# Placing of tokens split in two and moved within its round; GpSimd's list scatters read the tables themselves and are spread anew

## The chip, the cores and the metric

One core of a Trainium2 chip runs the whole program. The metric is device time in microseconds (us), the median of several executions. The engines are TensorE (PE), VectorE (DVE), ScalarE (ACT), GpSimd (POOL) and SyncE (SP); each runs its own program in order, and they meet at semaphores.

## What is computed

The input x has 16 x 512 tokens of 256 channels. All of it is normalised; then one branch is an RWKV layer over the 16 sequences of 512 tokens, the other a routed mixture of experts, and the output is x + s * silu(g).

```
def _L0_attn_ref(x, ...):
    x = _ln(x, ln0_w, ln0_b)
    h = _ln(x, ln1_w, ln1_b)
    xx = _time_shift(h)
    xk = h * tmk + xx * (1 - tmk)          # xv, xr alike
    k = jnp.einsum('btc,oc->bto', xk, Wk)  # v alike, sr with a sigmoid
    att = _wkv(w, time_first, k, v)        # recurrence over time
    x = x + jnp.einsum('btc,oc->bto', sr * att, Wo)
    h2 = _ln(x, ln2_w, ln2_b)
    ...
    kf = jnp.square(jax.nn.relu(jnp.einsum('btc,hc->bth', xk2, Wfk)))
    kv = jnp.einsum('bth,ch->btc', kf, Wfv)
    return x + jax.nn.sigmoid(...) * kv

def _L0_ffn_ref(x, Wg, W1, W2):
    probs = jax.nn.softmax(xt @ Wg, axis=-1)
    _, top_idx = jax.lax.top_k(probs.T, cap)     # each expert takes its best T // E tokens
    tok2exp = ...                                # one expert for each token
    for e in range(E):
        h = jax.nn.gelu(xt @ W1[e], approximate=False) @ W2[e]
        out = out + gate[:, None] * h
```

## The kernel before

The work goes in two stages. The first runs 16 rounds b = 0 to 15, one for each sequence of 512 tokens, and computes the RWKV layer; the second works off 72 tiles of 128 tokens, sorted by expert.

**A round.** On TensorE (`round_`, L936) round b does the hidden products of sequence b-1 (`hidden`, L887, lines 901, 903 and 908, eight groups of six), its `receptance` (L920, two halves), `turn1` of b+1 (transposes, L836), `channel_out(b-1, 0)` (L932), `project_out(b)` (L883), the projections k and v of b+1 (L871), another `channel_out`, `turn2(b)`, the projection r of b+1, and two more `channel_out`. `hidden` waits from its fourth group on for ScalarE's `relu` of three groups earlier; the second half of `receptance` waits for `relu` 6; `channel_out(b-1, 0)` waits for all eight squares.

On ScalarE (`round_`, L644) the order is: `logs(b)` (L599), relus and squares 0 and 1 and relu 2 of b-1 (L621, L625), `shares(b)` (L605, L608, with a load of function tables), relus 3 and 4, square 2, relu 5, `norm1(b+1)` (L530), relu 6, square 3, relu 7, squares 4 to 7, `affine1(b+1)`, and later `norm2(b)`, `norm0(b+2)`, `affine2(b)` (L538), `exp_past(b+1)`, `exponents(b+1)`, `split_mix(b)` and `exp_now(b+1)`. `norm1(b+1)` waits for GpSimd's `rstd1(b+1)`, `norm2(b)` for `rstd2(b)`.

On VectorE (`round_`, L1529, and `wkv`, L1449):

```
def wkv(b, extra, ahead, further):
    wkv_state(b)              # L1398, scans; ScalarE's logs wait for them
    embed_scale(b + 1); embed_shift(b + 1)
    extra(b, 0)
    wkv_gap(b)                # L1405; ScalarE's shares wait for it
    gate_out(b - 2); moments1(b + 1); residual2(b - 2)
    wkv_mix(b)                # L1416 to L1445, its end releases project_out
    extra(b, 1); fetch(b + 2)
```

(shortened) and then `mix1(b+1)`, `residual1(b)` with the second statistics (L1475, L1320, L1324), `extra(b, 2)`, `mix1_r(b+1)`, `wkv_start(b+1)` (L1384 to L1392), `extra(b, 3)` and `mix2(b)` (L1337, L1341, L1376). `extra` is a slot for the router's work, of which each round has four.

**Routing.** Rounds 0 to 3 take the logits and the softmax, rounds 3 to 11 search each expert's threshold bit by bit; round 11 (`SELECT_ROUND`) counts ties, selects, chooses an expert for each token, and keeps the prefix sums. In round 12 (`LIST_ROUND`), slot 0, `place_tokens` (L1239 to L1291) turns them into the row of the sorted list that each token takes: `place` (128 x 64) and `info` (128 x 64 x 4), and it ends by raising `routed`. `list_part` (L1294) then copies a quarter of both tables, 16 columns, to `place_cur` and `info_cur` (L1299, L1300), and again in slot 0 of rounds 13, 14 and 15, where it first waits until the scatters of the quarter before have landed.

**GpSimd.** Its round (L446) computes the reciprocal deviations of the norms, `rstd1(b+1)` and `rstd2(b)` (L426 to L431, four small instructions each), which wait for the statistics on VectorE. From round 12 on, `add_to_list` (L413) issues indirect DMAs (L419), each of which scatters one column of 128 tokens into `sorted_list` in HBM. There are 64. The order of rounds 12 to 14 is `rstd1(b+1)`, eight scatters, `rstd2(b)`, eight scatters; that of round 15 is sixteen scatters, `zero_rows` (L443, eight memsets, after a wait for the last `att_done`), `rstd2(15)`. Then come the gathers of the second stage.

**SP.** It issues the loads and stores of the rounds; after `routed` it loads W2, after all 64 scatters it loads the list back (L367) and then W1. VectorE's `first_indices` (L1519) waits for the list in round 15.

Of the kernel before, what the change touches and what calls it, by code (L numbers as in the profile page):

```python
# [28 lines left out]
I32 = mybir.dt.int32  # L29
F32R = mybir.dt.float32r  # L30
ALU = mybir.AluOpType
ACT = mybir.ActivationFunctionType
AX_X = mybir.AxisListType.X
ds = bass.ds

P = 128
# [34 lines left out]
def rwkv_times_moe(nc, x, xT, vec, ln0_w, ln0_b, WkT, WvT, WrT, WoT, WfkT, WfrT, WfvT, Wg, W1, W2,  # L71
# [19 lines left out]
    with ExitStack() as ctx:  # L91
# [19 lines left out]
        def sb(name, shape, dt=F32):  # L111
            return ctx.enter_context(nc.sbuf_tensor(name, shape, dt))
# [20 lines left out]
        place_cur = sb("place_cur", [P, LT], I32)  # L133
        info_cur = sb("info_cur", [P, LT, 4], I32)
# [103 lines left out]
        probs_turned routed pads_out list_cur list_scattered list_in w1_in w2_in w2_hi_done w2_first_done w2_split  # L238
# [140 lines left out]
        def _(pool):  # L379
# [33 lines left out]
            def add_to_list(b, half):  # L413

                wait_run(pool, S["list_cur"], b - (LIST_ROUND - 1))
                if isinstance(b, int) and b == LIST_ROUND:
                    pool.wait_ge(S["pads_out"], 16)
                for j in range(half * LT // 2, (half + 1) * LT // 2):
                    pool.indirect_dma_start(sorted_list[:, :], bass.IndirectOffsetOnAxis(place_cur[:, j:j + 1], axis=0),  # L419
                                            info_cur[:, j, :], None).then_inc(S["list_scattered"], 16)  # L420
# [25 lines left out]
            def round_(b, listing=False, ahead=True):  # L446
                if ahead:
                    rstd1(b + 1)
                if listing:
                    add_to_list(b, 0)  # L450
                if not ahead:
                    add_to_list(b, 1)
                    zero_rows()
                rstd2(b)
                if listing and ahead:
                    add_to_list(b, 1)
# [9 lines left out]
            round_(LIST_ROUND, listing=True)  # L466
            with pool.Fori(LIST_ROUND + 1, NB - 1) as b:
                round_(b, listing=True)
            round_(NB - 1, listing=True, ahead=False)
# [572 lines left out]
        def _(v):  # L1042
# [128 lines left out]
            def route(b, point):  # L1171
                if b == SELECT_ROUND:
                    (count_ties, select, choose, keep_prefix)[point]()
                elif point == 0:
                    place_tokens()
                    list_part(b)
# [62 lines left out]
            def place_tokens():  # L1239
# [7 lines left out]
                c8 = lambda k: tiny[:, 16 + k * E:16 + (k + 1) * E]  # L1247
# [10 lines left out]
                R.then(v.tensor_scalar(c8(5), c8(4), float(P), -1.0, ALU.mult, ALU.add))  # L1258

                R.then(v.tensor_tensor(work, work, logits, ALU.subtract))  # L1260
# [33 lines left out]
            def list_part(b):  # L1294

                n = b - LIST_ROUND
                if not (isinstance(b, int) and b == LIST_ROUND):
                    wait_run(v, S["list_scattered"], n * (16 * LT))
                v.tensor_copy(place_cur[:], place[:, ds(n * LT, LT)])  # L1299
                v.tensor_copy(info_cur[:].rearrange("p t w -> p (t w)"),  # L1300
                              info[:].rearrange("p t w -> p (t w)")[:, ds(n * (4 * LT), 4 * LT)].bitcast(I32)
                              ).then_inc(S["list_cur"], 1)

            def listing(b, point):
                if point == 0:
                    list_part(b)

# [263 lines left out]
            with v.Fori(LIST_ROUND + 1, NB - 2) as b:  # L1571
                round_(b, listing)
            round_(NB - 2, listing, further=False)
            round_(NB - 1, listing, ahead=False, further=False)
# [114 lines left out]
```

## Time and profile before

| | |
|---|---|
| runs shown, us | 1118.58, 1117.18, 1118.22 (median 1118.22) |
| profiled execution, us | 1113.32 |
| its span on the core, us | 1111.4 |
| mean granted TensorE clock | 0.978 of 2.4 GHz |
| TensorE busy | 92% |
| VectorE busy | 81% |
| ScalarE busy | 62% |
| GpSimd busy | 35% |

The profiled execution lies 4.9 us under the median. Its span runs from the first to the last instruction; 1.9 us of its time lie around the span. In the timeline a row gives the start and the length of one or more like instructions, and in brackets the idle time of the engine before them and who ended it. The ends of matmuls are modelled. The first stage ends near 812 us, the second fills the rest.

### The profile page before, as it was taken

The numbers are of one execution on the slowest core, as the hardware profiler recorded it, in microseconds if no ns is written. First come the engines' busy times: TensorE is split into PE (matmuls) and PEld (weight loads), VectorE is DVE, ScalarE is ACT, GpSimd is POOL, SyncE is SP. The second block draws the span as 40 slices with busy tenths as digits, with TensorE's granted clock in tenths as the row PEclk, the third lists the DMA queues.
The fourth block names the chain that finished last, engine by engine and source line by source line (L and its number), as shares of the span: only waits on it lengthen the run. The fifth ranks groups of instructions, "written<-read, shape, count | busy, mean of one in ns | idle before, by whom it ended". The sixth has DMA issues, their size and how long they took to land.

```text
span 1111.4 us, 20678 instructions
## 1 busy us (share of the span) xinstructions
PE 1024.8 (92%) x5440; PEld 837.4 (75%) x5441; DVE 900.9 (81%) x1997; ACT 689.5 (62%) x1233; POOL 387.2 (35%) x407
## 2 busy tenths in 40 slices
PE   5679999999999999999999699999897999999996
PEld 5357787776777767777776578677787999999996
DVE  5799889998988989888899969787445777777775
ACT  2648565686756858567585557658254666666654
POOL 3105414110101101011110265467705665666663
PEclk9879999999999999999999899999998999999999
DMA  9424230101101011010110101063503333333320
GB/s 303 153 78 128 78 112 19 39 28 30 57 0 57 11 46 57 0 57 0 57 58 0 45 14 57 1 189 116 202 12 90 102 106 102 105 102 108 98 63 16
DMA packets 60091, 80.50 MB, mean 72 GB/s; under 512 B 7806, under 2 KB 47359, under 8 KB 60034
## 3 DMA queue, kind: packets, MB, share of 16 engines
q1 hardware_dynamic: 48658, 54.69, 15.5%
q0 software_dynamic: 11392, 25.32, 7.8%
q8 instruction: 19, 0.31, 0.1%
q14 instruction: 22, 0.18, 0.1%
HBM read 65.17 MB, written 26.49 MB: 82 GB/s over the span
## 4 chain that ended last, share of the span: by engine, by line
PE 59%; DVE 18%; issue 7%; ACT 7%; POOL 6%; another core or an unknown queue 1%; DVEq 1%; DMA 1%; ACTq 0%; POOLq 0%
PE psKV L932 13%; PE psM L1003 12%; PE psM L871 9%; PE psM L883 5%; POOL sorted_list L419 2%; DVE arena L1398 2%; PE psM L920 2%; DVE arena L1341 2%; PE psT L836 2%; ACT arena L625 2%; PE psR L792 2%; PE psM L901 2%; PE psM L1015 2%; DVE bnst L1320 2%; ACT arena L530 2%
## 5 line engine op out<-in xcount | busy, mean ns | idle before, releaser
L932 PE MATMUL psKV<-arena 128*128 128x256 f32 x1024 | 232.7, 382 | 4.1 <-ACT arena L625 4.1
L932 PEld LDWEIGHTS psKV<-arena 128*128 128x128 f32 x1024 | 193.1, 191 | 43.9 <-issue 17.5
L426 POOL TENSOR_SCALAR lnw<-mv 128x4 f32<-128x4 f32 x32 | 19.0, 593 | 509.6 <-DVE mv L1324 509.5
L1003 PE MATMUL psM<-arena 128*128 128x128 f32 x1152 | 143.4, 278 | 0.7 <-issue 0.2
L1003 PEld LDWEIGHTS psM<-arena 128*128 128x128 f32 x1152 | 135.8, 194 | 3.1 <-issue 2.6
L901 PE MATMUL psM<-mix_hi,wfk_hi 128*128 128x512 f32 x256 | 106.5, 416 | 21.8 <-ACT arena L621 21.6
L577 ACT ACTIVATE arena<-psM 128x512 f32<-128x512 f32 x64 | 36.5, 590 | 130.4 <-PE psM L871 130.4
L487 POOL DMA_INDIRECT out_dram<-arena,out_idx x72 | 90.8, 1261 | 76.1 <-DVE row_idx L1512 36.4
L1341 DVE SCALAR_TENSOR_TENSOR arena<-arena,vecs 128x512 f32<-128x512 f32 x160 | 109.9, 745 | 0.0
L530 ACT ACTIVATE arena<-s_ring,cf 128x256 f32 (+1 forms) x128 | 66.5, 592 | 58.0 <-POOL cf L431 58.0
L903 PE MATMUL psM<-mix_hi,wfk_lo 128*128 128x512 f32 x256 | 101.0, 395 | 0.0
L621 ACT ACTIVATE arena<-psM 128x512 f32<-128x512 f32 x128 | 73.9, 589 | 35.2 <-PE psM L908 32.7
L740 ACT ACTIVATE arena<-psM 128x512 f32<-128x512 f32 x72 | 43.1, 599 | 69.9 <-PE psM L1003 49.6
L419 POOL DMA_INDIRECT sorted_list<-info_cur,place_cur x64 | 75.6, 1182 | 22.3 <-issue 20.5
L908 PE MATMUL psM<-mix_lo,wfk_hi 128*128 128x512 f32 x256 | 80.1, 394 | 0.4 <-DVE mix_lo L1376 0.4
L901 PEld LDWEIGHTS psM<-mix_hi,wfk_hi 128*128 128x128 f32 x256 | 48.6, 190 | 37.5 <-ACT arena L621 27.9
L474 POOL DMA_INDIRECT arena<-xs_rows,row_idx x64 | 68.4, 1068 | 22.1 <-issue 22.1
L625 ACT ACTIVATE arena<-arena 128x512 f32<-128x512 f32 x128 | 75.4, 627 | 0.9
L1590 DVE TENSOR_TENSOR hT_rounded<-arena,hT_rounded 128x512 fp32r<-128x512 f32 x72 | 49.5, 687 | 28.4 <-ACT hT_rounded L741 19.8
L883 PE MATMUL psM<-wo,arena 128*128 128x256 f32 x256 | 60.0, 389 | 5.1 <-DVE arena L1445 5.1
L920 PE MATMUL psM<-arena 128*128 128x256 f32 x256 | 60.1, 382 | 3.8 <-ACT arena L621 3.8
L1337 DVE TENSOR_TENSOR arena<-arena 128x512 f32<-128x512 f32 x64 | 41.7, 688 | 24.9 <-ACT arena L538 20.3
(208 smaller groups left out, 2417.9 us busy)
## 6 DMA issues: line engine op xcount, KB each, us to landing
desk<-in_x SPq DMA_DIRECT2D x16, 512.0 KB, 5.0
arena<-in_x SPq DMA_DIRECT2D x16, 512.0 KB
desk<-in_xT SPq DMA_DIRECT2D x16, 512.0 KB, 4.0
xs_rows<-s_ring SPq DMA_DIRECT2D x16, 512.0 KB
xs_rows<-in_x SPq DMA_DIRECT2D x16, 512.0 KB
desk<-in_W SPq DMA_DIRECT2D x8, 512.0 KB
arena<-in_W SPq DMA_DIRECT2D x8, 512.0 KB
out_dram<-arena,out_idx POOLq DMA_INDIRECT x72
```

The costliest lines, as they stand in the source:

```text
L419: pool.indirect_dma_start(sorted_list[:, :], bass.IndirectOffsetOnAxis(place_cur[:, j:j + 1], axis=0), info_cur[:, j, :], None).then_inc(S ...
L487: pool.indirect_dma_start(out[:, :], bass.IndirectOffsetOnAxis(out_idx[i][:, 0:1], axis=0), out_t[i], None, bounds_check=T - 1, oob_is_err ...
L530: ins = act.activation(hn[:, j], xs[:, j * C:(j + 1) * C], ACT.Identity, scale=cf[:, 0, j:j + 1], bias=cf[:, 1, j:j + 1])
L625: act.activation(kf2[:, h], kf2[:, h], ACT.Square).then_inc(S["sq_done"], 1)
L871: ins = pe.matmul(psM[:, u % 3, :], w[:, k, c * P:(c + 1) * P], mixA[:, m, k, :], start=(k == 0), stop=(k == CH - 1))
L883: ins = pe.matmul(psM[:, 1 + j // 2, (j % 2) * C:(j % 2 + 1) * C], att[:, c, j * P:(j + 1) * P], wo[:, c, :], start=(c == 0), stop=(c == C ...
L901: pe.matmul(psM[:, h % 3, :], wfk_hi[:, k, n], mix_hi[:, k, :], start=(k == 0), stop=False)
L903: pe.matmul(psM[:, h % 3, :], wfk_lo[:, k, n], mix_hi[:, k, :], start=False, stop=False)
L920: ins = pe.matmul(psM[:, (HC + u) % 3, (j % 2) * C:(j % 2 + 1) * C], mixB_r[:, k, j * P:(j + 1) * P], wfr[:, k, :], start=(k == 0), stop=( ...
L932: ins = pe.matmul(psKV[:, j // 2, (j % 2) * C:(j % 2 + 1) * C], kf2[:, h, j * P:(j + 1) * P], wfv[:, h, :], start=(h == 0), stop=(h == HC ...
L1003: ins = pe.matmul(psM[:, i % 2, f * P:(f + 1) * P], w1_t[i % 2][:, k, f * P:(f + 1) * P], xnT[i % 2][:, k, :], start=(k == 0), stop=(k == ...
L1341: return v.scalar_tensor_tensor(dst[:, c], dmix[:, c], vecs[:, c, V[m]:V[m] + 1], hT[:, c, 0:SEQ], ALU.mult, ALU.add)
```

## The change

`place_tokens` is cut in two. `expert_starts`, its first part (to the subtraction at L1260), runs in slot 2 of round 12, behind `residual1(12)` and its statistics; the rest runs in slot 3, behind `mix1_r(13)` and `wkv_start(13)`, ahead of `mix2(12)`. The arithmetic is the same. `list_part` and its two small tables are gone, with the semaphore `list_cur` and VectorE's waits on landed scatters in rounds 13 to 15; each scatter takes its column from `place` and `info`. GpSimd's order becomes: round 12 `rstd1(13)`, `rstd2(12)`, a wait for `pads_out` and `routed`, 16 scatters; round 13 `rstd1(14)`, 8 scatters, `rstd2(13)`, 16 scatters; round 14 `rstd1(15)`, 8, `rstd2(14)`, 16; round 15 `zero_rows`, `rstd2(15)`.

```
-            def add_to_list(b, half):
-
-                wait_run(pool, S["list_cur"], b - (LIST_ROUND - 1))
-                if isinstance(b, int) and b == LIST_ROUND:
-                    pool.wait_ge(S["pads_out"], 16)
-                for j in range(half * LT // 2, (half + 1) * LT // 2):
-                    pool.indirect_dma_start(sorted_list[:, :], bass.IndirectOffsetOnAxis(place_cur[:, j:j + 1], axis=0),
-                                            info_cur[:, j, :], None).then_inc(S["list_scattered"], 16)
+            def add_to_list(first, last):
+
+                for t in range(first, last):
+                    pool.indirect_dma_start(sorted_list[:, :], bass.IndirectOffsetOnAxis(place[:, t:t + 1], axis=0),
+                                            info[:, t, :].bitcast(I32), None).then_inc(S["list_scattered"], 16)
...
-            def round_(b, listing=False, ahead=True):
+            def round_(b, mid=(0, 0), late=(0, 0), ahead=True):
                 if ahead:
                     rstd1(b + 1)
-                if listing:
-                    add_to_list(b, 0)
-                if not ahead:
-                    add_to_list(b, 1)
+                    add_to_list(*mid)
+                else:
                     zero_rows()
                 rstd2(b)
-                if listing and ahead:
-                    add_to_list(b, 1)
+                if isinstance(b, int) and b == LIST_ROUND:
+                    pool.wait_ge(S["pads_out"], 16)
+                    pool.wait_ge(S["routed"], 1)
+                add_to_list(*late)
...
-            round_(LIST_ROUND, listing=True)
-            with pool.Fori(LIST_ROUND + 1, NB - 1) as b:
-                round_(b, listing=True)
-            round_(NB - 1, listing=True, ahead=False)
+            q = NTILE // 8
+            round_(LIST_ROUND, late=(0, 2 * q))
+            round_(LIST_ROUND + 1, mid=(2 * q, 3 * q), late=(3 * q, 5 * q))
+            round_(LIST_ROUND + 2, mid=(5 * q, 6 * q), late=(6 * q, 8 * q))
+            round_(NB - 1, ahead=False)
...
                 if b == SELECT_ROUND:
                     (count_ties, select, choose, keep_prefix)[point]()
-                elif point == 0:
+                elif point == 2:
+                    expert_starts()
+                elif point == 3:
                     place_tokens()
-                    list_part(b)
...
+            def expert_starts():
+                v.wait_ge(S["route_pe"], 4)
+
+                R.then(v.tensor_copy(et(logits), psR[:].rearrange("p (t e) -> p e t", e=E)))
+                R.wait()
+                R.then(v.tensor_tensor_scan(work, reset, logits, 0.0, ALU.mult, ALU.add))
...
+                R.then(v.tensor_scalar(c8(5), c8(4), float(P), -1.0, ALU.mult, ALU.add))
+                R.then(v.tensor_tensor(work, work, logits, ALU.subtract))
+
             def place_tokens():
...
-                R.then(v.tensor_tensor(work, work, logits, ALU.subtract))
                 R.wait()
...
-            def list_part(b):
-
-                n = b - LIST_ROUND
-                if not (isinstance(b, int) and b == LIST_ROUND):
-                    wait_run(v, S["list_scattered"], n * (16 * LT))
-                v.tensor_copy(place_cur[:], place[:, ds(n * LT, LT)])
-                v.tensor_copy(info_cur[:].rearrange("p t w -> p (t w)"),
-                              info[:].rearrange("p t w -> p (t w)")[:, ds(n * (4 * LT), 4 * LT)].bitcast(I32)
-                              ).then_inc(S["list_cur"], 1)
-
-            def listing(b, point):
-                if point == 0:
-                    list_part(b)
-
+            def plain(b, point):
+                pass
...
             with v.Fori(LIST_ROUND + 1, NB - 2) as b:
-                round_(b, listing)
-            round_(NB - 2, listing, further=False)
-            round_(NB - 1, listing, ahead=False, further=False)
+                round_(b, plain)
+            round_(NB - 2, plain, further=False)
+            round_(NB - 1, plain, ahead=False, further=False)
```

## Rows read from the trace of the kernel before

**Rows 1.** The page: TensorE's busy line, and the group of the list's scatters.

```profile
PE 1024.8 (92%) x5440; PEld 837.4 (75%) x5441; DVE 900.9 (81%) x1997; ACT 689.5 (62%) x1233; POOL 387.2 (35%) x407
...
L419 POOL DMA_INDIRECT sorted_list<-info_cur,place_cur x64 | 75.6, 1182 | 22.3 <-issue 20.5
```

**Rows 2.** Timeline of TensorE, 600 to 800 us (start, us, what, idle before).

```profile
633.07 0.79 PE L901 MATMUL psM<-mix_hi,wfk_hi 128*128 128x512 f32 x1 [10.07 <-ACT arena L621]
...
638.35 3.68 PE L920 MATMUL psM<-arena 128*128 128x256 f32 x16
...
680.78 0.50 PE L901 MATMUL psM<-mix_hi,wfk_hi 128*128 128x512 f32 x1 [0.97 <-ACT arena L621]
...
683.66 3.62 PE L920 MATMUL psM<-arena 128*128 128x256 f32 x16
...
687.99 3.62 PE L932 MATMUL psKV<-arena 128*128 128x256 f32 x16
...
792.03 1.95 PE L836 MATMUL psT<-cst,arena 128*128 128x128 f32 x8 [4.12 <-ACT arena L530]
```

**Rows 3.** Windows: PE, PEld, DVE, ACT, POOL busy; granted clock; DMA share; GB/s.

```profile
633.00:639.00 6.00, 5.93 (x15) 4.71 (x16) 6.00 (x11) 5.00 (x11) 4.66 (x6) 0.54 0.68 201
```

**Rows 4.** Timeline of VectorE, 560 to 832 us.

```profile
617.66 0.68 DVE L1242 COPY desk<-psR 128x512 f32<-128x512 f32 x1
...
620.75 0.68 DVE L1260 TENSOR_TENSOR desk<-desk 128x512 f32<-128x512 f32 x1
...
627.65 0.15 DVE L1291 COPY desk<-desk 128x1 f32<-128x1 f32 x1
...
640.79 1.29 DVE L1445 SCALAR_TENSOR_TENSOR arena<-arena 128x512 f32<-128x512 f32 x2
...
645.13 2.73 DVE L1341 SCALAR_TENSOR_TENSOR arena<-arena,vecs 128x512 f32<-128x512 f32 x4
...
663.70 1.36 DVE L1337 TENSOR_TENSOR arena<-arena 128x512 f32<-128x512 f32 x2 [5.24 <-ACT arena L538]
...
669.01 2.34 DVE L1398 TENSOR_TENSOR_SCAN arena<-arena 128x512 f32<-128x512 f32 x2
...
677.59 0.38 DVE L1324 BATCH_NORM_AGGREGATE mv<-bnst 128x2 f32<-128x6 f32 x4
...
787.19 0.38 DVE L1324 BATCH_NORM_AGGREGATE mv<-bnst 128x2 f32<-128x6 f32 x4
```

**Rows 5.** Timeline of ScalarE, 600 to 730 us.

```profile
628.68 1.28 ACT L605 ACT_TABLE_LOAD   x1 [9.10 <-DVE arena L1405]
...
670.34 1.28 ACT L599 ACT_TABLE_LOAD   x1 [0.88 <-DVE arena L1398]
...
676.38 1.28 ACT L605 ACT_TABLE_LOAD   x1
...
682.11 2.08 ACT L530 ACTIVATE arena<-s_ring,cf 128x256 f32 x4
```

**Rows 6.** Timeline of GpSimd, 500 to 800 us.

```profile
640.81 1.50 POOL L419 DMA_INDIRECT sorted_list<-info_cur,place_cur  x1 [0.30 <-issue]
...
646.41 0.96 POOL L419 DMA_INDIRECT sorted_list<-info_cur,place_cur  x1 [0.30 <-issue]
...
698.37 0.49 POOL L426 TENSOR_SCALAR lnw<-mv 128x4 f32<-128x4 f32 x1 [4.44 <-DVE mv L1324]
...
703.50 1.16 POOL L419 DMA_INDIRECT sorted_list<-info_cur,place_cur  x1 [0.53 <-issue]
...
712.76 2.23 POOL L419 DMA_INDIRECT sorted_list<-info_cur,place_cur  x1 [0.31 <-issue]
...
723.41 0.96 POOL L426 TENSOR_SCALAR lnw<-mv 128x4 f32<-128x4 f32 x1 [8.42 <-DVE mv L1324]
...
726.11 0.20 POOL L431 TENSOR_TENSOR cf<-lnw,cf 128x4 f32<-128x4 f32 x1 [0.18 <-POOL cf L429]
...
787.93 0.25 POOL L426 TENSOR_SCALAR lnw<-mv 128x4 f32<-128x4 f32 x1
```

More of the change, by code:

```diff
@@ L132, in rwkv_times_moe @@
         stats_cur = sb("stats_cur", [P, J, 2])
-        place_cur = sb("place_cur", [P, LT], I32)
-        info_cur = sb("info_cur", [P, LT, 4], I32)
         bnst = sb("bnst", [P, J, 6])
@@ L237, in rwkv_times_moe @@
         var_ready pow_ready bit_step bit_counted bit_summed route_step route_pe route_exp_in route_exp_out
-        probs_turned routed pads_out list_cur list_scattered list_in w1_in w2_in w2_hi_done w2_first_done w2_split
+        probs_turned routed pads_out list_scattered list_in w1_in w2_in w2_hi_done w2_first_done w2_split
         x_in x_out s_out fetched x0_ready scaled0 embedded moments_step ln1_stats cf1_ready hn1_ready tr1_done
@@ L1237, in keep_prefix @@
                 assert R.k == R_KEPT, R.k
-            def place_tokens():
+            c8 = lambda k: tiny[:, 16 + k * E:16 + (k + 1) * E]
+            def expert_starts():
                 v.wait_ge(S["route_pe"], 4)
@@ L1245, in place_tokens @@
                 R.wait()
-                c8 = lambda k: tiny[:, 16 + k * E:16 + (k + 1) * E]
                 R.then(v.tensor_scalar(c8(0).bitcast(I32), et(work)[:, :, NTILE - 1], float(P - 1), None, ALU.add))
@@ L1260, in place_tokens @@
                 R.then(v.tensor_tensor(work, work, logits, ALU.subtract))
+            def place_tokens():
                 R.wait()
```

## The prediction

> **What bounds the kernel now.** I read the page first. TensorE is busy for 92% of the span [rows 1], so a round is worth what it makes TensorE stop for. Then the timeline of TensorE: in a common round it stops once, for 0.97 us in the hidden products, at 680.78; in round 12 it stops at the same place for 10.07 us, at 633.07 [rows 2]. ScalarE's timeline says why: its shares waited 9.10 us for VectorE's gap, L1405 [rows 5]. VectorE's says what stood ahead of the gap: the placing, 617.66 to 627.80 (L1242 to L1291) [rows 4]. The products behind the stop ran slow as well: from 633.07 to the receptance at 638.35 they took 5.28 us, where the same ones took 2.88 (680.78 to 683.66) [rows 2]; the granted clock there was 0.54, the lower of the two levels, 1.2 GHz, for most of the stretch [rows 3].
>
> All times below are on the axis of this trace; what is won in round 12 is taken off at the end.
>
> **1. What leaves slot 0 of round 12.** The stop shrinks from 10.07 to 0.97, 9.1 us, and the slow clock behind it goes, 5.28 - 2.88 = 2.4. Nothing else is late there: ScalarE was waiting for the gap alone, and the statistics and `norm1(13)` follow the gap as in a common round. **Gain 11.5 us.** Bounds: 9.1, if the clock falls for another cause, and 11.5.
>
> **2. What slots 2 and 3 get.** The first part lasts 617.66 to 621.43, 3.77 us, the rest 6.37 [rows 4]. VectorE has a hole there: it idled 5.24 us until 663.70, when `mix2(12)` began, so its work before ended at 658.46 [rows 4]. With 10.14 us put in, `mix2(12)` starts at 668.6, 4.9 late. `mix1_r` and `wkv_start(13)` slip by 3.8 at most; their readers (the r projection, `exp_past`) start from 661 on, so I cost that at nothing; were that cover gone it would be under 1 us. Behind `mix2` come the scans of `wkv_state(13)`, at 669.01 before, 673.9 now. ScalarE's logs begin 1.33 us behind them (670.34 [rows 5]), at 675.2, and its shares 6.04 behind that (676.38 [rows 5]), less some 0.5 of waits for TensorE, which is now ahead: 680.7. The seventh of the eight hidden groups waits for relu 3, which stands behind the shares, so TensorE resumes at 685.1 instead of 680.78: **4.3 us lost**; the late start of the hidden products, some 1.7 us, is within it. Bounds 3.3 (`affine2` could come earlier, and VectorE's hole with it) and 4.9.
>
> **3. GpSimd's queue behind `routed`.** `routed` rises at 668.6. Behind the wait stand 16 scatters, and behind these `rstd1(14)`, on which `norm1(14)` waits in the middle of ScalarE's relus and squares. A scatter costs 1.18 us and 0.30 between two, 1.48 [rows 1, 6]; the first starts 0.3 behind the signal. The sixteenth ends at 668.9 + 23.7 = 692.6. The statistics that `rstd1(14)` needs were there at 677.97 [rows 4], 682.9 now: GpSimd comes 10 us late. `rstd1` took 2.9 us beside a busy VectorE (723.41 to 726.31 [rows 6]); VectorE is nearly through by then, I take 2.6. `norm1(14)` starts at 695.3 instead of 682.11 [rows 5]. From `norm1` to `channel_out(12, 0)` it was 687.99 - 682.11 = 5.9 us, squares in between [rows 2, 5]; so TensorE reaches that product at 701.2 instead of 688.0, 13.2 late. It will have stopped for about 8 us ahead of the second half of `receptance`. A stop of 10.07 and one of 4.12 us were each followed by slow products (eight transposes in 1.95 us at 792.03) [rows 2], so the clock falls here too, on 2.6 us of work (half of `receptance`, `turn1`) that starts 3.5 us ahead of 701.2: 1.6 more. **Loss 14.8 us, with the 4.3 of step 2 in it.** Bounds: scatters undisturbed, 0.96 + 0.30 = 1.26 [rows 6], give 9.7 and 0 to 1 of clock; all at 1.50 + 0.30 give 18.3 and 2.
>
> **4. Rounds 13 and 14.** The list needs the same 64 scatters, but 16 late ones now stand between `rstd2(13)` and `rstd1(15)`. From the start of `rstd2(13)` to the first scatter it was 5.13 us (698.37, 703.50), eight scatters took 11.49 (703.50 to 714.99) [rows 6], so sixteen end 28.1 us after the start. `rstd1(15)` was due 25.04 after it (723.41): 3.1 late. `rstd1(14)` ended, a period of 45.24 us before 726.31 (the statistics at 677.97 against 723.2), at 681.07 and `norm1(14)` began at 682.11: 1.0 of slack. **2.1 lost**; bounds 0 (scatters at 1.26 end 25.3 after) and 5. The eight in the middle fit: `rstd2` follows `rstd1` by 20.2 us (678.2 to 698.37), and three and 11.5 are needed.
>
> **5. The end.** In round 15 the scatters, `zero_rows` and `rstd2(15)` (787.93 [rows 6]) followed each other; the second statistics were ready at 787.57 [rows 4], 0.36 us before. The last scatters now end near 772, and SP's list and W1 loads start some 7 us sooner, with nothing waiting for them. **Gain 0.3.** The six copies and three waits of `list_part` in rounds 13 to 15 lie in VectorE's spare time: nothing.
>
> Sum: -11.5 + 14.8 + 2.1 - 0.3 = **+5.1 us**. The sum stands on the profiled execution (1113.32 us, 1.9 around the span); it lies 4.9 under the median shown, and I carry the difference over: 1118.2 + 5.1 = **1123.3**. A measurement of this kernel can tell some 0.2% (2.2 us) from no change.
>
> **A rule against the trace.** A scatter took 0.96 us beside L1341 (646.41) but 1.50 beside L1445 (640.81), both with two inputs in SBUF [rows 4, 6]; the price thus hangs on the neighbour only in part, and the mean holds both. The Trainium skill, GPSIMD Engine Reference, Key points, says that GpSimd shares its SBUF interfaces with VectorE and that instructions with two SBUF inputs contend with it. By that rule alone nearly all of the 16 would be stretched. This trace bears it out in some rows and not in others.
>
> **Rivals.**
> - *The scatters run short.* Out of the new place many of them stand beside `mix2`, the embedding and the gap, where some were at 0.96. At 1.26 each: -11.5 + 9.7 + 1 + 0 - 0.3 = -1.1, so 1117.1. For it: the 0.96 at 646.41 [rows 6]. Against: `wkv_mix`, beside whose end the 1.50 stands, falls in the same stretch. Chance 0.22.
> - *Faster: GpSimd's queue does not reach the path.* The place is `norm1(14)`. If its coefficients come by 686.4 (682.11 + 4.3), only step 2 remains: -11.5 + 4.3 - 0.3 = -7.5, 1110.7 us. That takes 16 scatters in 686.4 - 2.6 - 668.9 = 14.9 us, 0.93 each; from there the price rises by 16 us for each us of a scatter, and even lies at some 1.28. No row has less than 1.26, which speaks against; but GpSimd's times are the roughest of the trace, and with scatters near 1.26, no fall of the clock and a smaller step 2 the time already lies 3 us below. Chance 0.18.
> - *Every scatter is stretched.* At 1.80 each step 3 costs 5.1 more (16 x 0.32) and step 4 some 3 more: +13, 1131 us. For it: rows at 1.50 [rows 6]; against: the rows at 0.96, and eight in 11.49. Chance 0.07.
> - *The forecast*, 0.53.
>
> **Numbers.** Slower by over 0.2%: 0.53 + 0.07 = 0.60; within: 0.22; faster: 0.18. The range leaves out the full price of the second rival and of the third. Its lower end is 1116.0 (scatters at 1.26 and no fall of the clock: -2.1), its upper 1127.5 (4.2 above the forecast: half of the way to the stretched scatters).
>
> **What the new profile would show.** Right: no stop of 10 us in round 12; VectorE without idle time ahead of `mix2(12)`; a stop of TensorE of 2 to 3 us ahead of the seventh hidden group of round 13; sixteen scatters in a row of about 23.7 us and `norm1(14)` idle for some 9 us with GpSimd's L431 as releaser; TensorE stopped about 8 us in `receptance` with a low granted clock behind it; one wait for L431 of 2 us in round 14. Wrong: sixteen scatters in under 19 us; `norm1(14)` waiting for nothing; or a stop in round 12 that stays, for then something else than the placing held the shares.

## The result, and the profile of the changed kernel

The changed kernel took 1129.07 us (median of 4 runs, 1127.15 to 1131.43), the kernel before 1118.4 (4 runs, 1117.18 to 1118.92): ratio 1.0096, with 95% confidence between 1.0074 and 1.0118. That is 10.7 us slower, where 5.1 were forecast. The profiled execution took 1127.15 us for a span of 1125.2, 13.8 more than the profiled execution of before.

From the page, answering to [rows 1]:

```profile
PE 1030.4 (92%) x5440; PEld 841.2 (75%) x5441; DVE 900.4 (80%) x1989; ACT 689.5 (61%) x1233; POOL 379.9 (34%) x407
...
L414 POOL DMA_INDIRECT sorted_list<-info,place x64 | 72.3, 1130 | 32.1 <-issue 18.7
```

A scatter is a little shorter than before (1130 against 1182 ns), and GpSimd has a new wait of 13.4 us (32.1 - 18.7) ahead of this group. TensorE is busy 5.6 us longer (1030.4 against 1024.8) for the same 5440 products, at a mean clock of 0.974 against 0.978; VectorE and ScalarE are not busy for longer. The rest of the 13.8 us is waits. The timeline of TensorE, 600 to 810 us, answering to [rows 2]:

```profile
624.24 0.50 PE L897 MATMUL psM<-mix_hi,wfk_hi 128*128 128x512 f32 x1 [0.99 <-ACT arena L617]
...
660.74 0.47 PE L897 MATMUL psM<-mix_hi,wfk_hi 128*128 128x512 f32 x1 [0.70 <-ACT mix_hi L610]
...
673.01 0.49 PE L897 MATMUL psM<-mix_hi,wfk_hi 128*128 128x512 f32 x1 [2.28 <-ACT arena L617]
...
687.37 3.74 PE L916 MATMUL psM<-arena 128*128 128x256 f32 x8 [8.04 <-ACT arena L617]
...
726.32 0.50 PE L897 MATMUL psM<-mix_hi,wfk_hi 128*128 128x512 f32 x1 [1.51 <-issue]
...
734.94 0.50 PE L897 MATMUL psM<-mix_hi,wfk_hi 128*128 128x512 f32 x1 [2.70 <-ACT arena L617]
...
802.17 1.09 PE L832 MATMUL psT<-cst,arena 128*128 128x128 f32 x8 [3.78 <-ACT arena L526]
```

Round 12 has only the common stop of 0.99 us at 624.24 left of the 10.07 at 633.07 before. In round 13 stand a stop of 2.28 us ahead of the seventh hidden group and one of 8.04 in `receptance`. Two further stops of over 1 us stand in round 14 (726.32 and 734.94). The last line is the end, 4.12 before and 3.78 now.

The windows of TensorE, answering to [rows 3] (columns: stretch; length and busy time of PE, PEld, DVE, ACT, POOL; granted clock; DMA share; GB/s):

```profile
633.00:639.00 6.00, 6.00 (x28) 5.08 (x27) 4.00 (x7) 1.14 (x3) 0.00 (x0) 1.00 0.01 1
682.00:692.00 10.00, 4.63 (x17) 3.80 (x18) 0.00 (x0) 5.63 (x11) 8.02 (x11) 0.66 0.02 1
732.00:737.00 5.00, 2.30 (x8) 1.64 (x7) 4.28 (x6) 5.00 (x10) 4.08 (x4) 0.83 0.96 287
737.00:740.00 3.00, 3.00 (x11) 2.42 (x10) 3.00 (x6) 2.75 (x6) 2.39 (x3) 0.71 1.11 369
```

The stretch of the axis that stood at 0.54 before now has the full clock. It holds other products now; the ones that ran slow before start at 624.24 and reach the receptance in 2.87 us (5.28 before). Three other stretches have lost the clock: behind the stops at 687 and 735, and behind the one at 673.01, where the products up to the receptance take 4.44 us in place of 2.88.

VectorE's timeline, 655 to 675 us, answering to [rows 4], and ScalarE's, 660 to 740 us, answering to [rows 5]:

```profile
656.92 0.15 DVE L1290 COPY desk<-desk 128x1 f32<-128x1 f32 x1
656.99 1.28 DVE L1324 TENSOR_TENSOR arena<-arena 128x512 f32<-128x512 f32 x2
...
670.44 0.38 DVE L1311 BATCH_NORM_AGGREGATE mv<-bnst 128x2 f32<-128x6 f32 x4
```

```profile
668.62 1.28 ACT L601 ACT_TABLE_LOAD   x1
...
684.77 2.07 ACT L526 ACTIVATE arena<-s_ring,cf 128x256 f32 x4 [10.33 <-POOL cf L426]
...
725.67 0.60 ACT L617 ACTIVATE arena<-psM 128x512 f32<-128x512 f32 x1 [4.57 <-PE psM L904]
...
727.73 0.60 ACT L617 ACTIVATE arena<-psM 128x512 f32<-128x512 f32 x1 [0.80 <-remote]
...
729.93 0.60 ACT L617 ACTIVATE arena<-psM 128x512 f32<-128x512 f32 x1 [0.94 <-remote]
```

GpSimd's timeline, 640 to 735 us, answering to [rows 6]:

```profile
657.97 1.39 POOL L414 DMA_INDIRECT sorted_list<-info,place  x1 [13.42 <-DVE desk L1290]
659.66 1.44 POOL L414 DMA_INDIRECT sorted_list<-info,place  x1 [0.30 <-issue]
661.41 2.63 POOL L414 DMA_INDIRECT sorted_list<-info,place  x1 [0.30 <-issue]
664.34 1.99 POOL L414 DMA_INDIRECT sorted_list<-info,place  x1 [0.30 <-issue]
666.63 0.96 POOL L414 DMA_INDIRECT sorted_list<-info,place  x1 [0.30 <-issue]
...
681.56 0.96 POOL L414 DMA_INDIRECT sorted_list<-info,place  x1 [0.30 <-issue]
682.59 0.20 POOL L421 TENSOR_SCALAR lnw<-mv 128x4 f32<-128x4 f32 x1
...
727.74 2.01 POOL L414 DMA_INDIRECT sorted_list<-info,place  x1 [0.30 <-issue]
729.82 0.20 POOL L421 TENSOR_SCALAR lnw<-mv 128x4 f32<-128x4 f32 x1
```

Placing ends at 657.07 and `mix2(12)` follows at once, with no idle time in between. Sixteen scatters then fill 657.97 to 682.52, and `rstd1(14)` stands behind them although its statistics were ready at 670.82 (670.44 + 0.38). So `norm1(14)` waits 10.33 us. The chain is as forecast. The new thing is at 725.67: ScalarE's first relu of round 14 waits 4.57 us, where in e8, another run of the same program, it waits 1.08 for the same products. The next two relus have waits with the releaser "remote", which stands here where the profile names no engine and no queue of the program.

**Counting by rounds.** The clearest measure is the distance between two starts of `residual1`'s addition on VectorE (L1475 before, L1462 after). All runs of this study stand in the table, each against the kernel before on its own chip. "Sum" is the sum of the four distances less 193.3, the sum of the profile of before.

```
run              chip  round 12  13     14     15     sum   us        before    ratio   95%
before           -     58.69     45.25  45.24  44.15  -     1118.4
changed          -     47.13     60.40  51.89  44.15  +10.2 1129.07   1118.4    1.0096  1.0074 to 1.0118
e5_before        4     58.80     45.23  45.23  44.17  +0.1  1091.31   (one run)
e1_again         15    47.16     61.87  46.24  44.15  +6.1  1094.0    1090.49   1.0033  1.0021 to 1.0044
e2_first16       15    47.12     60.07  45.20  44.19  +3.3  1093.78   1090.49   1.0031  1.0018 to 1.0043
e3_second16      15    47.13     50.19  46.23  44.18  -5.6  1083.92   1090.49   0.9933  0.9912 to 0.9954
e4_spread        15    47.14     50.35  45.19  44.22  -6.4  1081.62   1090.49   0.9919  0.9898 to 0.994
e6_slot0         4     57.49     49.43  46.26  44.17  +4.0  1093.93   1090.42   1.003   1.002 to 1.004
e7_slot0_spread  4     57.44     45.22  45.21  44.18  -1.3  1089.3    1090.42   0.9988  0.9975 to 1.0001
e8_again         4     47.13     61.15  46.23  44.20  +5.4  1093.92   1090.42   1.0028  1.0016 to 1.0039
e9_tiles_later   10    47.12     49.72  48.74  44.62  -3.1  1121.33   1125.14   0.9963  0.9942 to 0.9984
e10_spread2      10    47.12     50.37  47.26  44.17  -4.4  1122.15   1125.14   0.9977  0.9954 to 0.9999
e11_again        10    47.12     61.68  51.79  44.21  +11.5 1134.29   1125.14   1.0091  1.0068 to 1.0114
e12_exit13       2     47.13     60.85  47.89  44.18  +6.7  1096.89   1089.67   1.0068  1.0051 to 1.0084
e13_first16b     2     47.17     61.51  45.27  44.19  +4.8  1092.71   1089.67   1.0023  1.001 to 1.0036
e14_second16b    2     47.17     48.77  46.24  44.16  -7.0  1083.37   1089.67   0.9946  0.9924 to 0.9967
e15_exit13       5     47.16     60.57  47.88  44.17  +6.5  1096.52   1091.44   1.0047  1.0012 to 1.0082
e16_first16      5     47.12     60.46  45.20  44.18  +3.6  1095.15   1091.44   1.0032  1.0014 to 1.005
e17_tiles_later  12    47.14     50.76  47.30  51.92  +3.8  1122.82   1124.92   0.9981  0.995 to 1.0013
e18_exit13       12    47.17     61.27  47.90  44.21  +7.2  1128.69   1124.92   1.0046  1.0022 to 1.007
```

Two things are to be seen before any experiment is read. First, the kernel before takes about 1090 us on chips 15, 4, 2 and 5 and 1118 to 1125 on chips 10 and 12 and on the one of the forecast. Its rounds 12 to 15 are the same on both sorts (58.69 and 58.80, then 45.2). Second, a round's distance says more than the total: for one program it repeats within 0.1 us in round 12 and within 1.5 in round 13, where the clock moves it.

### The profile page after: what moved, and what is told of

It reads as the page before. It is cut to its first block, busy times and chain, and to the rows that moved or that the text cites. A ratio compares the mean times of both kernels' runs of the same rounds, so it can differ in the third digit from the quotient of the medians.

```text
span 1125.2 us, 20636 instructions
## 1 busy us (share of the span) xinstructions
PE 1030.4 (92%) x5440; PEld 841.2 (75%) x5441; DVE 900.4 (80%) x1989; ACT 689.5 (61%) x1233; POOL 379.9 (34%) x407
## 4 chain that ended last, share of the span: by engine, by line
PE 58%; DVE 18%; issue 11%; ACT 6%; POOL 4%; DMA 1%; another core or an unknown queue 1%; DVEq 1%; ACTq 0%; SPq 0%; POOLq 0%
PE psKV L928 12%; PE psM L999 10%; PE psM L867 9%; PE psM L879 5%; PE psM L916 2%; DVE arena L1385 2%; DVE arena L1328 2%; POOL sorted_list L414 2%; PE psT L832 2%; PE psR L788 2%; PE psM L897 2%; DVE bnst L1307 2%; PE psR L1011 2%; PE psM L1011 2%; PE psM L904 2%
## 5 line engine op out<-in xcount | busy, mean ns | idle before, releaser
L999 PEld LDWEIGHTS psM<-arena 128*128 128x128 f32 x1152 | 136.8, 194 | 5.3 <-issue 5.0
L414 POOL DMA_INDIRECT sorted_list<-info,place x64 | 72.3, 1130 | 32.1 <-issue 18.7
L1577 DVE TENSOR_TENSOR hT_rounded<-arena,hT_rounded 128x512 fp32r<-128x512 f32 x72 | 49.7, 690 | 36.2 <-ACT hT_rounded L737 19.9
L470 POOL DMA_INDIRECT arena<-xs_rows,row_idx x64 | 70.9, 1107 | 22.0 <-issue 19.7
L916 PEld LDWEIGHTS psM<-arena 128*128 128x128 f32 x256 | 49.1, 194 | 22.4 <-ACT arena L617 15.2
```

The lines of the kernel that those rows point to most:

```text
L916: ins = pe.matmul(psM[:, (HC + u) % 3, (j % 2) * C:(j % 2 + 1) * C], mixB_r[:, k, j * P:(j + 1) * P], wfr[:, k, :], start=(k == 0), stop=( ...
L999: ins = pe.matmul(psM[:, i % 2, f * P:(f + 1) * P], w1_t[i % 2][:, k, f * P:(f + 1) * P], xnT[i % 2][:, k, :], start=(k == 0), stop=(k == ...
```

## The experiments

The expectations use short names: Q is the forecast's account, that GpSimd's queue behind `routed` holds `rstd1`; the others are named in them.

**Is it the number of scatters ahead of `rstd1`?** e1 runs the changed kernel again. e2, e3 and e4 change nothing but where the list is split:

```
-            round_(LIST_ROUND, late=(0, 2 * q))
-            round_(LIST_ROUND + 1, mid=(2 * q, 3 * q), late=(3 * q, 5 * q))
-            round_(LIST_ROUND + 2, mid=(5 * q, 6 * q), late=(6 * q, 8 * q))
e2:
+            round_(LIST_ROUND, late=(0, 16))
+            round_(LIST_ROUND + 1, mid=(16, 24), late=(24, 32))
+            round_(LIST_ROUND + 2, mid=(32, 42), late=(42, 8 * q))
e3:
+            round_(LIST_ROUND, late=(0, 8))
+            round_(LIST_ROUND + 1, mid=(8, 16), late=(16, 32))
+            round_(LIST_ROUND + 2, mid=(32, 42), late=(42, 8 * q))
e4:
+            round_(LIST_ROUND, late=(0, 8))
+            round_(LIST_ROUND + 1, mid=(8, 19), late=(19, 31))
+            round_(LIST_ROUND + 2, mid=(31, 42), late=(42, 8 * q))
```

> The changed kernel once more, with nothing altered, to see what of its profile repeats. Time between two starts of the residual addition on VectorE (the round period; 45.25 us for rounds 13 and 14 of the kernel before): in the first profile of the changed kernel it was 60.4 us for round 13 and 51.9 for round 14. Theory Q (both losses come from GpSimd's queue: 16 scatters ahead of rstd1): 60.4 and 51.9 again, within 0.5. Rival F (the stall of 4.6 us of ScalarE at the start of round 14, for which the profile names no releaser behind its first wait, is a chance of one execution): 60.4, but round 14 at 47 or less. Median near 1129 us under Q; under F the profiled time would lie some 5 us under the other runs.

> The changed kernel, with 16 scatters ahead of rstd1(14) as it has them, but only 8 late ones in round 13 (8 ahead of rstd1(15)); the others moved to round 14. Q: round 13 stays at 60.4, round 14 falls from 51.9 to 45.3 to 46; in all some 6 us less than the changed kernel, 1122 to 1124. Rival F2 (round 14's loss is one of starting the program's code behind ScalarE's and VectorE's loops and has nothing to do with the scatters): round 14 stays near 51.9, no change in time.

> The changed kernel with 8 scatters ahead of rstd1(14) in place of 16, and 16 ahead of rstd1(15) as it has them. Q: rstd1(14) starts when its statistics are there; round 13 falls from 60.4 to 45.25 + 4.1 = 49.4, with the late start of the shares alone left; round 14 stays at 51.9; in all 11 us less than the changed kernel, near 1118. Rival P (the placing in slots 2 and 3 costs TensorE most of the 15 us of round 13 whatever GpSimd does): round 13 stays above 56. F2: as Q for round 13.

> The changed kernel with the scatters spread so that none stands in the way of a wanted rstd: 8 late in round 12, 11 and 12 in round 13, 11 and 22 in round 14. Q: round 13 at 49.4, round 14 at 45.3 to 46; time = before - 11.5 + 4.1 - 0.3, 7 to 8 us under the kernel before, 1110 to 1112. F2: round 14 near 51.9 and a time near 1117. P: no faster than before.

Measured: round 13 costs 60.07 and 61.87 us with 16 scatters ahead of `rstd1(14)` (e2, e1), and 50.19 and 50.35 with 8 (e3, e4). Round 14 costs 46.23 and 46.24 with 16 ahead of `rstd1(15)` (e3, e1), and 45.19 and 45.20 with 8 or 12 (e2, e4). With the rest of the change in all four kernels, each of the two places follows the scatters ahead of it, and Q holds for round 13: the second eight of the first sixteen are worth some 10 us. For round 14 it gives 1.0 us. The 51.9 that Q expected there in e1 and e3 did not come, so the first result's other 5.6 us are not the wait for `rstd1(15)`. Spread otherwise, the change is a gain of 0.8% on this chip (e4), and of 0.2% on chip 10 (e10, below). Timelines of e4_spread, GpSimd, TensorE and ScalarE from 668 to 722 us:

```profile
669.40 0.96 POOL L414 DMA_INDIRECT sorted_list<-info,place  x1 [0.30 <-issue]
670.43 0.53 POOL L421 TENSOR_SCALAR lnw<-mv 128x4 f32<-128x4 f32 x1
```

```profile
671.98 0.50 PE L897 MATMUL psM<-mix_hi,wfk_hi 128*128 128x512 f32 x1 [2.26 <-ACT arena L617]
...
718.77 0.50 PE L897 MATMUL psM<-mix_hi,wfk_hi 128*128 128x512 f32 x1 [0.96 <-ACT arena L617]
```

```profile
673.31 2.07 ACT L526 ACTIVATE arena<-s_ring,cf 128x256 f32 x4
```

With eight scatters `rstd1(14)` starts at 670.43 and `norm1(14)` waits for nothing. The stop of 2.26 us ahead of the seventh group stays, so it belongs to the placing in slots 2 and 3, not to GpSimd (e7 below, with the same split and the placing in slot 0, has 45.22 in round 13). In e4 it is what is left of round 13's extra 5.1 us (50.35 - 45.25), with the slow clock behind it: the seventh group restarts 3.5 us late, and the products from there to the receptance take 4.45 us in place of 2.88.

e13 and e14 repeat e2 and e3 on another chip.

> 16 scatters ahead of rstd1(14) and only 8 late ones in round 13 (the kernel of e2), which end before ScalarE leaves its loop. G and H both, on a chip of the second kind: no scatter runs at the start of round 14, so the stall is gone and round 14 takes 45.2 to 46. Rival J (the stall comes from round 14's own code wherever the scatters are, and the kernel before escapes it by chance): 50 or more. On a chip of the first kind 45.2, as in e2.

> 8 scatters ahead of rstd1(14), 16 late ones in round 13 (the kernel of e3). On a chip of the second kind G and H: round 13 at 50.2, round 14 at 51 to 52 with the stall, 3 us or less under the kernel before or over it; on one of the first kind 50.2 and 46.2, 6 us under it.

Measured: 61.51 and 45.27 for e13, 48.77 and 46.24 for e14, which is the same pattern. The 1.4 us between e14 and e3, one program, are the clock: behind the same stop (2.28 and 2.27 us) and the same restart, the products up to the receptance take 2.86 us in e14 and 4.29 in e3.

**The parts of the change alone.** e6 keeps GpSimd's new order and puts the placing back into slot 0; e7 adds the split of e4 to that; e5 is the kernel before, e8 the changed one.

```
-                elif point == 2:
+                elif point == 0:
                     expert_starts()
-                elif point == 3:
                     place_tokens()
```

> The kernel before, unaltered, for a profile of it on the chip of these runs. Theory C (the first profile of the changed kernel had one stall of some 5.6 us in round 14 that belongs to its chip, not to the change): this profile has round periods of 58.7, 45.25, 45.25 and 44.15 us for rounds 12 to 15, and its second stage shows none of the waits without a named releaser that the profile of step 1 has (10 us and more on ScalarE's lines).

> The changed kernel with the placing put back whole into slot 0 of round 12 (one part of the change undone); GpSimd's order as changed, 16 scatters behind rstd2(12). Theory Q (the loss of round 13 comes from 16 scatters that can only start behind the placing in slot 3): round 12 back at 58.7 us; routed is up long before rstd2(12), so the scatters start near 655 and end near 679, 1 to 2 us behind the time at which rstd1(14) is wanted: round 13 at 45.3 to 47, round 14 at 46.2 as in the changed kernel. Time: that of the kernel before within 2 us. Rival P (16 late scatters cost the same wherever the placing stands): round 13 at 56 or more, 10 us over the kernel before.

> Placing in slot 0 as before, scatters straight from the tables and spread 8, 11 and 12, 11 and 22: what the new spread is worth without the move. Q: round 12 at 58.7, rounds 13 and 14 at 45.25, and at the end of round 15 rstd2 is no longer behind the scatters, 0.3 us and what TensorE's clock makes of it (0 to 2 us): 0 to 2.5 us under the kernel before. Rival: the copies and waits of the old list on VectorE were worth something in rounds 13 to 15: a period under 45.0, 3 us or more gained.

> The changed kernel a third time, beside the kernel before. Theory C: round 14 at 46.2 us again, no stall without a releaser in the first stage, and 3 to 5 us over the kernel before if the chip is the one of the last runs. If the chip is one that runs the kernel before in 1118 us: then unnamed stalls in both profiles, and the difference tells whether the changed kernel has more of them (over 8 us) or not (3 to 5).

e6 missed: 45.3 to 47 us were expected for round 13, and 49.43 came. Timelines of e6_slot0, GpSimd and TensorE from 655 to 690 us:

```profile
655.62 1.36 POOL L414 DMA_INDIRECT sorted_list<-info,place  x1 [0.45 <-issue]
...
677.47 0.97 POOL L414 DMA_INDIRECT sorted_list<-info,place  x1 [0.30 <-issue]
678.51 0.82 POOL L421 TENSOR_SCALAR lnw<-mv 128x4 f32<-128x4 f32 x1
...
685.24 3.15 PE L916 MATMUL psM<-arena 128*128 128x256 f32 x8 [2.22 <-ACT arena L617]
```

Even with the placing in its old slot the sixteen fill 22.8 us (655.62 to 678.44), hold `rstd1(14)`, and stop TensorE for 2.22 us, with slow products behind (eight of the receptance in 3.15 us, where sixteen take 3.62 at the full clock); sixteen in a row are too many in either place. Round 12 was expected at 58.7 and took 57.49. e7, without the sixteen, is 0.12% faster than before, less than can be told, and 1.4 us shorter in round 12 than e5 (57.44 against 58.80): so much of round 12's gain comes without moving the placing. The rest is the freeing of slot 0 (e4 against e7: 10.3 us of round 12, less 5.1 of round 13).

**The rest of step 2.** The seventh group waits for relu 3 behind the shares. e9 splits the list as e4, moves the last part of the placing, which finds the expert of each tile (L1283 to L1288), into slot 3 of round 13 and lets GpSimd wait only for what the scatters read, so that `mix2(12)` could come 1.8 us earlier.

```
-                    pool.wait_ge(S["routed"], 1)
+                    pool.wait_ge(S["route_step"], R_PLACED)
...
+                assert R.k == R_PLACED, R.k
+            def expert_tiles():
...
+            def tiles(b, point):
+                if point == 3:
+                    expert_tiles()
...
-                round_(b, plain)
+                round_(b, tiles)
```

> The spread list of e4, and the last part of the placing (which expert each tile belongs to, three instructions, 1.9 us) moved on to slot 3 of round 13; the scatters wait for the table alone. Theory Q, as it stands now: mix2(12) is late by 3.0 us in place of 4.9, the seventh hidden group of round 13 restarts 1.6 late in place of 3.5, and a stop that short leaves TensorE's clock up: round 13 at 46.5 to 47.5 us in place of 50.35; round 14 at 45.2, its hole in VectorE takes the 1.9. 3 us under e4. Rival: the sum of the work in VectorE decides, wherever it stands: round 13 and 14 together stay at 95.5.

> The spread list of e4 again, to stand beside e9 on one chip and to narrow its interval: 7 to 9 us under the kernel before on a chip without unnamed stalls, periods of 50.3 and 45.2 in rounds 13 and 14.

> The changed kernel once more. Theory C (the stall of step 1 in round 14 is not the change's): 46.2 us in round 14, 60 to 62 in round 13, 3 to 4 us over the kernel before. Rival: over 8 us again.

e9 missed: round 13 took 49.72 us and not 46.5 to 47.5. Timelines of e9_tiles_later, TensorE, VectorE and ScalarE from 665 to 690 us:

```profile
670.64 0.50 PE L897 MATMUL psM<-mix_hi,wfk_hi 128*128 128x512 f32 x1 [2.27 <-ACT arena L617]
...
689.10 3.53 PE L867 MATMUL psM<-arena,wk 128*128 128x512 f32 x4 [2.45 <-DVE s_ring L1468]
...
687.73 1.22 DVE L1468 TENSOR_TENSOR s_ring<-s_ring,psM 128x1024 f32<-128x1024 f32 x1 [4.76 <-remote]
...
688.46 0.60 ACT L573 ACTIVATE arena<-psM 128x512 f32<-128x512 f32 x1 [7.89 <-remote]
```

What the edit was made for came: the stop ahead of the seventh group is as long as before (2.27), but TensorE starts again only 1.7 us late (32.63 us behind the addition of round 12, against 30.93 in the kernel before and 34.46 in e4), and the clock stays up. What was not foreseen is further on. VectorE's own `residual1(13)`, from whose start the round is counted, waits 4.76 us without a named releaser, where the same addition waits 2.00 in e10 on the same chip, and TensorE waits for it. The parts add up: 45.25 + 1.7 + 2.8 = 49.7. In e17, the same program on chip 12, the restart is 1.7 late as well, the slow clock takes 1.6, and the same addition waits 4.24 us: 45.25 + 1.7 + 1.6 + 2.2 = 50.8, measured 50.76. So the rival, that the sum of VectorE's work decides, fails for the restart. Against e10, e9 gains 0.65 us of round 13 and loses 1.5 of round 14; the totals (0.9963 and 0.9977) overlap. The program was never run on a chip of the 1090 us sort, and no gain of time over e4 is shown.

**The 5.6 us of round 14.** e11, the changed kernel on chip 10, has round 14 at 51.79 as in the first result (51.89), where e1 and e8 have 46.24 and 46.23. So theory C falls, that the stall was a chance of the first profile: the same program loses 5.6 us more on one sort of chip. ScalarE's timelines from 716 to 730 us, first of e11_again, then of e8_again:

```profile
718.25 1.26 ACT L595 ACTIVATE arena<-arena 128x512 f32<-128x512 f32 x2
725.77 0.60 ACT L617 ACTIVATE arena<-psM 128x512 f32<-128x512 f32 x1 [6.26 <-remote]
726.40 0.63 ACT L621 ACTIVATE arena<-arena 128x512 f32<-128x512 f32 x1
728.69 0.60 ACT L617 ACTIVATE arena<-psM 128x512 f32<-128x512 f32 x1 [1.66 <-PE psM L904]
```

```profile
719.17 1.26 ACT L595 ACTIVATE arena<-arena 128x512 f32<-128x512 f32 x2
721.51 0.60 ACT L617 ACTIVATE arena<-psM 128x512 f32<-128x512 f32 x1 [1.08 <-PE psM L904]
```

Behind the same logs the same relu starts 1.08 us later on one chip and 6.26 on the other. ScalarE's loop runs to round 13 (`Fori(BIT_ROUND, NB - 2)`, L700) and round 14 is written out behind it: this relu is near the start of code that runs for the first time. Two theories: the stall is ScalarE's entry into that code while scatters run (G), or it is the scatters alone, whatever ScalarE runs (H); the sixteen run until 729.8 in the changed kernel, and before, eight were over at 714.99. To tell them apart, ScalarE's loop ends a round earlier and all else stays:

```
-            with act.Fori(BIT_ROUND, NB - 2) as b:
+            with act.Fori(BIT_ROUND, NB - 3) as b:
                 round_(b)
+            round_(NB - 3)
```

> The changed kernel, with ScalarE's loop ended one round earlier (round 13 written out, with the same instructions), so that ScalarE has left its loop long before round 14. There are two kinds of chip: one with the kernel before at 1090 us, where round 14 of the changed kernel takes 46.2 us, and one with it at 1118 to 1125, where ScalarE's first relu of round 14 stands still for 5 us with no named releaser and the round takes 51.8. Theory G (on chips of the second kind new program code reaches ScalarE late where it leaves a loop while GpSimd's scatters run): round 14 falls to 46.2 to 48, and a stall may appear at the start of round 13, partly under the wait for rstd1(14). Rival H (the scatters in flight hold up ScalarE there whatever it fetches): round 14 stays at 51.8. On a chip of the first kind: 60 to 62 and 46.2, no difference to the changed kernel.

> The kernel of e12 again, in the hope of a chip of the sort that runs the kernel before at 1118 to 1125 us. There, G: round 14 at 46 to 48 us (e12 showed 47.9 on a chip of the other sort); H: 51.8 or more, with ScalarE's first relu of round 14 standing still. On the other sort nothing new: 60.9 and 47.9.

> The kernel of e2 and e13 again, for the same reason: on a chip of the slower sort round 14 at 45.2 to 46 if the scatters at the loop's end have a part in the stall (G, H), 50 or more if not (J). On the other sort 45.2.

> The kernel of e9 (spread list, the tiles' experts in slot 3 of round 13) again. On a chip of the faster sort Q gives round 13 at 46.5 to 48.5 us (e9 had 49.7 there with a stall of unnamed origin in it), round 14 at 45.2, and 9 to 11 us under the kernel before; the rival (the sum of VectorE's work decides) 95.5 for both rounds and 7 to 9 us, as e4.

> The kernel of e12 and e15 once more. On a chip of the slower sort G: round 14 at 46 to 49 us; H: 51.8. On the faster sort 60.9 and 47.9.

e12 and e15 fell on chips of 1090 us, where there is no stall to remove; they show the price of the edit itself, round 14 at 47.89 and 47.88. e18 fell on one of 1125 us. Its ScalarE and GpSimd timelines, 716 to 735 us:

```profile
721.59 0.60 ACT L617 ACTIVATE arena<-psM 128x512 f32<-128x512 f32 x1 [1.08 <-PE psM L905]
...
733.46 2.08 ACT L526 ACTIVATE arena<-s_ring,cf 128x256 f32<-128x256 f32 x4 [2.77 <-POOL cf L426]
...
725.88 0.95 POOL L414 DMA_INDIRECT sorted_list<-info,place  x1 [0.30 <-issue]
```

The relu waits 1.08 us as on the other sort, with the scatters still running beside it, and round 14 takes 47.90, as in e12 and e15. The whole costs 1.0046 and not 1.0091 to 1.0096. So H falls, as far as one profile and eight runs on chip 12 can tell (the changed kernel itself was not run there): scatters beside that relu are not enough for a stall. G is not shown by this. ScalarE now leaves its loop into round 13, with sixteen scatters running there too, and the first relu of that round, at 663.67, waits for nothing; a stall of some us would stand in this row whatever `norm1(14)` waits for later. That instructions are loaded late is a guess: no row names the load.

Whether it takes both, the exit and the scatters beside it (G), or only round 14's own code (J), is open. Against J, round 14 is written out in e18 as well and has no stall. That the scatters have a part is suggested by this: in the kernel before the same exit cost nothing (1.08 us) with the scatters over by 714.99, as the round began; in e9, e10 and e17, where twelve stand in that place, the relu waited 3.59, 3.49 and 3.53 us and started 0.9 to 1.0 us behind the end of the twelfth, and with sixteen (the first result and e11) it waited 4.57 and 6.26. Against G stands round 13 of e18. e16 was meant for this and fell on a chip of 1090 us. Nor is the exit the only such place, nor ScalarE the only such engine: e9 and e17 have VectorE's 4.76 and 4.24 us in round 13, and e17 has 51.92 in round 15, with a wait of ScalarE of 3.01 <-remote at 772.53. All of these are on chips of the slower sort; the profiles on the others have no wait for "remote" at all.

## Why the prediction missed

**Step 1, right.** Forecast 11.5 us; round 12 went from 58.69 to 47.13, 11.56. The stop of 10 us is gone, and the products that had a clock of 0.54 behind it run at full speed. Not all of it is the move's: in e7, with the placing in slot 0, the stop is 9.87 us, the products behind it take 4.28 in place of 5.28, and the round is already 1.4 shorter than in e5.

**Step 2, the wait right, its size near by luck.** VectorE has no hole ahead of `mix2(12)`, and the stop ahead of the seventh group is there. The restart is late by 3.5 us, forecast 4.3 (the two stops of 0.70 and 0.62 ahead of it are in this). Left out was the clock: the products behind a stop of 2.3 us ran slow for 1.5 more in e3 and e4, where the stop stands alone and costs 4.9 and 5.1 in all, above the upper bound or at it. In e14 it costs 3.5, the restart alone. Of the sixteen profiles with this stop (2.23 to 2.28 us) nine have the slow products and seven do not, the same program among both; what decides it was not found. The forecast had counted a slow clock behind stops of 10 and 4 us alone.

**Step 3, right, in part by luck.** Forecast 14.8 us for round 13 with step 2 in it; 15.15 came (60.40 - 45.25), and 15.9 to 16.6 in e8, e11 and e1, the same program. The sixteen took 24.55 us (forecast 23.7), the first one 0.9 behind `routed` (forecast 0.3), `rstd1` 1.9 (forecast 2.6), `norm1(14)` idled 10.33 (about 9), and TensorE stopped 8.04 in `receptance` (about 8; 10.17 in e8, where the products ahead of it ran at the full clock) with a clock of 0.66 over the stretch. The mechanism is the forecast's; its terms missed by up to 0.9 us each and partly cancelled.

**The rule weighed there.** By the trace the first four scatters took 1.39 to 2.63 us, next to `mix2`, the scan and the embedding, and nine of the other twelve 0.96, some of them next to instructions of VectorE that also read two tiles of SBUF (L1421 to L1432). The Trainium skill, GPSIMD Engine Reference, Key points, would stretch nearly all of them; the trace agrees for the first four and not for those nine, and the rival that stands on it, 1131 us, has its time nearly right by luck: its price of 1.80 us for a scatter did not come, and a stall that it does not know filled the gap.

**Step 4, the one that failed.** It said of round 14: "2.1 lost; bounds 0 (scatters at 1.26 end 25.3 after) and 5". Measured were 6.65 us (51.89 - 45.24). On chips of 1090 us it is 1.0 (e1, e3, e8), and `norm1(15)` idled 0.91 to 0.94, so the queue was even priced too high. The other 5.6 us are ScalarE's stall, the wait of 4.57 us at 725.67 and the ones behind it, near the exit of its loop. The step did not have it and put nothing in its place: it priced only the wait for `rstd1(15)`, and asked of each late instruction who waits for it, but not what else the late scatters now run beside. In e18, with the exit moved, the stall is gone; its cause stays open. The profile of before did hold a sign of it, in its table of waits of ScalarE (who waited, for whom, us in total, times, longest):

```profile
ACT arena L748 <- remote: 10.4, 4, 4.6
...
ACT arena L740 <- remote: 7.6, 5, 2.6
```

These 18.0 us without a named releaser stand in the second stage; e5, the same program on a chip of 1090 us, has none. An engine of that chip could stall for some us with nothing of the program to explain it, and the upper end of the range, 1127.5, had no room for one more.

**Step 5, right.** Forecast 0.3 us; the stop ahead of `turn2(15)` went from 4.12 to 3.78.

**The sum.** Rounds 12 to 15 make -11.56 + 15.15 + 6.65 + 0 = +10.24, and the end -0.34, so +9.9 between the two profiles. These lie 13.8 us apart (1111.4 and 1125.2) and the medians 10.7. Of the 3.9 left, 0.3 stand ahead of round 12 and 3.6 behind the end, in the second stage, where the change alters no work; both profiles have waits for "remote" there, and what makes the 3.6 was not settled. Without the stall of round 14 the rounds and the end make +4.3, against 5.1 forecast, and the chips of 1090 us, which have no stall, show +3.5 (1.0033 and 1.0028). There the rounds sum to +6.1 and +5.4 and the total is some 2 us less; the difference lies behind round 15, where the clock at `turn2` also differs between two executions of one program, and this too was not settled.

## What to carry to other kernels

Count what stands ahead of the next urgent instruction on a queue: here eight scatters ahead of `rstd1` cost nothing and sixteen cost 10 us, so a moved block of issues should be cut to the slack of what stands behind it, and measured by the distance between two rounds rather than by the total. A stop of 2.3 us can have a price beyond its length: slow products followed it in nine profiles of sixteen, for 1.4 to 1.6 us, so both cases belong in the range. Where a profile has waits without a named releaser, look on which chip they occur, leave room for one more in the range, and repeat the comparison on a second chip before one number is believed.

## What was not expected of the hardware

Chips of one kind differ by 3% in the time of one program: 1089.67 to 1091.44 us for the kernel before on four, 1118.4 to 1125.14 on chips 10 and 12 and in the first comparison, whose chip the record does not name. The first stage takes the same time on both (round 15's addition at 784.49 us in the profile of before, at 785.03 in e5); in the second, ScalarE has waits for "remote" on the latter alone, 18.0 us in two lines of the profile of before. On such a chip the changed kernel costs 0.9 to 1.0%, on the others 0.3%.

The same relu, behind the end of ScalarE's loop and beside scatters of GpSimd, waited 4.57 and 6.26 us on the slower sort of chip and 1.08 on the other (e8); the round was 5.6 us longer. Why is open.

The granted clock of TensorE behind a stop of 2.23 to 2.28 us fell in nine profiles and stayed at 1.00 in seven, the same program among both (from the restart to the receptance 0.64 in e3, 1.00 in e14).

A scatter from GpSimd holds its queue for 0.96 us at least (0.95 in some rows), with 0.30 between two, and for up to 2.64 (e14); sixteen in a row took 22.8 us (e6) and 24.55.
